# Attention and ternary FFN on one core: the FFN of a batch moved into the next batch's step

## What is computed

```python
# attention: 16 heads of 16 channels
q = xn @ Wq.T; latent = xn @ Wkv_down.T; k = latent @ Wk_up.T; v = latent @ Wv_up.T
att = softmax(where(mask, q k / 4, -inf))     # band of 64 keys, and the first 4 keys ("sinks")
y = (att v) @ Wo.T
# ffn: two "bit linears", weights ternarized
def bitlinear(x, w):
    n = layer_norm(x)                         # over the row
    return n @ (sign(round(w / mean|w|)) * mean|w|).T
h = gelu(bitlinear(xn, w_fc))                 # (256, 1024) a batch
ffn = bitlinear(h, w_proj)                    # (256, 256) a batch
```

## Time and profile before

| | |
|---|---|
| median of 3 runs | 192.17 us (191.29 to 192.31) |
| the profiled execution | 193.13 us, of which the span of its instructions 191.2 us |
| TensorE (PE) busy | 147.9 us (77%), 2166 products |
| DVE busy | 111.3 us (58%) |
| ACT busy | 83.8 us (44%) |
| POOL busy | 34.0 us (18%) |
| mean granted TensorE clock | 0.911 of full |
| the chain that ended last | PE 54%, DVE 26%, ACT 10%, issue 3%, DMA 3% of the span |

### The profile page before, as it was taken

How to read it: one execution, slowest core, us unless ns; L and a number is a source line. 1 busy time by engine, 2 the same in 40 slices (tenths; PEclk the granted TensorE clock), 3 DMA queues, 4 the chain that set the end, 5 groups by cost and what they waited for, 6 DMA issues and landing times.

```text
span 191.2 us, 4928 instructions
## 1 busy us (share of the span) xinstructions
PE 147.9 (77%) x2166; PEld 103.6 (54%) x2166; DVE 111.3 (58%) x190; ACT 83.8 (44%) x124; POOL 34.0 (18%) x64
## 2 busy tenths in 40 slices
PE   1627930979799991998999929997999289989823
PEld 1415710446678760547888604476887144778711
DVE  0359799985750467657814675658025777380461
ACT  1656710456936222347762223369532205596100
POOL 6421491000073000200460001101210002003000
PEclk9999995599979999799999985999999759999987
DMA  5997000010000000040000000300000003000001
GB/s 172 304 347 186 23 2 0 3 54 6 0 0 3 3 3 0 24 140 3 3 2 3 3 0 0 110 3 3 0 3 3 2 3 110 0 3 0 3 3 55
DMA packets 7969, 7.61 MB, mean 40 GB/s; under 512 B 2564, under 2 KB 7592, under 8 KB 7848
## 3 DMA queue, kind: packets, MB, share of 16 engines
q1 hardware_dynamic: 6236, 6.05, 10.4%
q10 hardware_dynamic: 1712, 1.25, 2.1%
HBM read 6.24 MB, written 1.05 MB: 38 GB/s over the span
## 4 chain that ended last, share of the span: by engine, by line
PE 54%; DVE 26%; ACT 10%; issue 3%; DMA 3%; ACTq 1%; POOL 1%
PE acc L1000 8%; PE ring L937 7%; DVE rden L695 7%; PE ring L867 7%; PE aux L1036 6%; PE acc L1026 4%; ACT gh L407 3%; DVE mx L650 3%; DMA wvu_r<-in_L_attn_Wv_up 3%; PE ring L980 3%; PE ring L920 3%; DVE KL L630 3%; PE aux L855 2%; PE ring L989 2%; PE acc L1018 2%
## 5 line engine op out<-in xcount | busy, mean ns | idle before, releaser
L920 PE MATMUL ring<-mask,idb 128*128 128x384 bf16 (+1 forms) x48 | 15.4, 410 | 18.5 <-DVE vs L642 16.3
L421 ACT ACTIVATE E<-ring,un 128x1024 f32<-128x1024 f32 x16 | 17.7, 1112 | 6.2 <-PE ring L980 6.2
L655 DVE TENSOR_REDUCE mx<-ring 128x4 f32<-128x768 f32 x16 | 14.9, 953 | 6.0 <-PE ring L925 5.5
L625 DVE SCALAR_TENSOR_TENSOR Q<-qh,rowlo,ring 128x1024 f16<-128x1024 f16 x4 | 5.1, 1277 | 21.9 <-ACT qh L434 21.9
L452 ACT ACTIVATE yhT<-y 128x256 f16<-128x256 f32 x8 | 3.3, 416 | 31.9 <-DVE y L700 31.9
L920 PEld LDWEIGHTS ring<-mask,idb 128*128 128x128 bf16 x48 | 3.6, 108 | 22.1 <-ACT V L444 10.9
L1000 PE MATMUL acc<-prT,gh 128*128 128x256 f16 x64 | 15.5, 285 | 0.0
L1000 PE MATMUL acc<-prT,glo 128*128 128x256 f16 x64 | 15.3, 284 | 0.0
L317 POOL TENSOR_TENSOR ob<-att,xff 128x512 f32<-128x512 f32 x3 | 3.8, 1263 | 56.7 <-issue 37.8
L394 ACT ACTIVATE gl<-ring,a 128x1024 f32<-128x1024 f32 x8 | 8.9, 1113 | 10.0 <-PE ring L937 9.9
L689 DVE SCALAR_TENSOR_TENSOR glo<-ring,gam_r,gh 128x1024 f16<-128x1024 f32 x8 | 9.9, 1279 | 5.8 <-ACT gh L407 5.8
(11 more groups left out here) (187 smaller groups left out, 390.5 us busy)
## 6 DMA issues: line engine op xcount, KB each, us to landing
wfc_r<-in_L_ffn_w_fc SPq DMA_DIRECT2D x1, 1024.0 KB, 8.1
wpr_r<-in_L_ffn_w_proj SPq DMA_DIRECT2D x1, 1024.0 KB, 10.4
xres<-in_L_attn_x SPq DMA_DIRECT2D x4, 256.0 KB, 2.8
out<-ob SPq DMA_DIRECT2D x4, 256.0 KB, 2.1
bias<-in_c_bias SPq DMA_DIRECT2D x1, 825.0 KB
xin<-in_L_attn_x ACTq DMA_DIRECT2D x3, 256.0 KB, 2.8
wq_r<-in_L_attn_Wq ACTq DMA_DIRECT2D x1, 256.0 KB, 3.3
xin<-in_L_attn_x SPq DMA_DIRECT2D x1, 256.0 KB, 3.8
```

The lines of the kernel that those rows point to most:

```text
L421: nc.scalar.activation(E[:, 2 * gp:2 * gp + 2, 2 * tp:2 * tp + 2, :].rearrange("p g t q -> p g (t q)"), slot("p2", b, r)[:], ACT.Exp, scal ...
L655: nc.vector.tensor_reduce(out=o, in_=src[:, :, 0:2 * (T - BLK)].rearrange("p a (t k) -> p a t k", t=2), axis=AX.X, op=ALU.max).then_inc(re ...
L920: nc.tensor.matmul(s[:, a, 0:n * len(heads)].rearrange("p (t k) -> p t k", t=len(heads)), idb[:], mask[:].unsqueeze(1).to_broadcast([P, le ...
```

## The change

Step b keeps the back part of batch b and the front part of b + 1, but the FFN in it is now that of batch a = b - 1. Step 0 has no FFN; in its place the ternary weights are made there. The last step has two FFNs: that of batch 2 and that of batch 3. In detail:

- The row operands `xhT`, `xlT` get three buffers, and `a1` two, since they are read one step later.
- PE's order in steps 1 and 2: `maxima_transposed`, rows, sinks, `window_scores` 0, 1, latents, `window_scores` 2, `fc_tile(a, 0)`, `window_scores` 3, `fc_tile(a, 1)`, q, values 0, k, values 1, v, `hidden_transposed(a, 0)`, round 0 of the maxima, `hidden_transposed(a, 1)`, round 1, `second_product(a, 0)`, rounds 2 and 3, `second_product(a, 1)`, rounds 4 and 5, `output_product(b)`. The last product moves from ahead of round 3 to behind round 5, and into `acc`.
- `ORDER` follows, so the ring's waits change: q waits for `gelu(a, 0)`, the second transposed tile for `sink_values`, round 1 for the low half of tile 0, round 3 for that of tile 1.
- ACT and DVE: `hidden` behind the last exponential, `hidden_high` behind `values_moved`, `hidden_low` ahead of maxima 0 and 1. POOL's `residual(b - 1)` and `result(b - 1)` stand at the end of step b, and ACT's `attended(b)` behind the FFN's evacuation.
- Weights: the magnitudes of `w_fc` are summed on DVE and of `w_proj` on ACT (they swap), the two means are taken apart, both `is_lt` compares are on POOL; `first_ternary` on DVE stands in step 0 ahead of the queries, `second_ternary` behind maxima 0, with their transposes on ring places of their own.
- The last step ends with `second_product` of batch 3 in a ring place; DVE adds the attention part into `xff` and then scales and adds per tile, and SP stores two halves.

```diff
-                fc_tile(b, 0)
-                fc_tile(b, 1)
                 maxima_transposed(b)
-                if more:
-                    transposed_rows(b + 1)
+                if f < B:
+                    transposed_rows(f)
                 sink_scores(b)
-                hidden_transposed(b, 0)
-                hidden_transposed(b, 1)
                 window_scores(b, 0)
                 window_scores(b, 1)
-                if more:
-                    latents(b + 1)
-                second_product(b, 0)
+                if f < B:
+                    latents(f)
                 window_scores(b, 2)
-                second_product(b, 1)
+                if b:
+                    fc_tile(a, 0)
                 window_scores(b, 3)
...
+                if f < B:
+                    q_products(f)
+                    values(b, 0)
+                    k_products(f)
+                    values(b, 1)
+                    v_products(f)
+                    if b:
+                        hidden_transposed(a, 0)
+                        window_maxima(f, 0)
+                        hidden_transposed(a, 1)
+                        window_maxima(f, 1)
+                        second_product(a, 0, acc[:, 0:C])
+                        window_maxima(f, 2)
+                        window_maxima(f, 3)
+                        second_product(a, 1, acc[:, C:2 * C])
+                    else:
+                        first_ternary()
+                        window_maxima(f, 0)
+                        window_maxima(f, 1)
+                        second_ternary()
+                        window_maxima(f, 2)
+                        window_maxima(f, 3)
+                    window_maxima(f, 4)
+                    window_maxima(f, 5)
+                    output_product(b)
+                else:
+                    values(b, 0)
+                    hidden_transposed(a, 0)
+                    values(b, 1)
+                    hidden_transposed(a, 1)
+                    fc_tile(b, 0)
+                    fc_tile(b, 1)
+                    second_product(a, 0, acc[:, 0:C])
+                    second_product(a, 1, acc[:, C:2 * C])
+                    output_product(b)
+                    hidden_transposed(b, 0)
+                    hidden_transposed(b, 1)
+                    last_bank = take("F2", b)
+                    for i in range(TT_):
+                        second_product(b, i, last_bank[:, i, 0:C])
```

The last step on DVE, and POOL's loop:

```diff
+                    normalised(b, 0)
+                    hidden_low(a, 0)
+                    attended_low(b, 0)
+                    normalised(b, 1)
+                    hidden_low(a, 1)
+                    attended_low(b, 1)
+                    hidden_stats(b, 0)
+                    hidden_stats(b, 1)
+                    last_attended(b)
+                    hidden_low(b, 0)
+                    hidden_low(b, 1)
+                    last_result(b, 0)
+                    last_result(b, 1)
...
+            def last_attended(b):
                 wait(dve, mm_wo, b)
+                wait(dve, ld_res, b)
+                wait(dve, o_ok, b - 1)
...
+                first_scale(b)
                 if b + 2 < B:
                     row_factors(b + 2)
+                if b:
+                    second_scale(b - 1)
+                    residual(b - 1)
+                    result(b - 1)
+            second_scale(B - 1)
```

More of the change, by code:

```diff
@@ new lines, in maxima_slots, with score_slots, fc_slot, hidden_slot @@
+        def maxima_slots(f, rounds):
+            return [("f_p1", f, r, [(red1, f, r + 1)] + ([(red1s, f, 1)] if r == 5 else [])) for r in rounds]
+        def score_slots(b, rounds):
+            return [("p2", b, r, [(ex, b, r + 1)]) for r in rounds]
+        def fc_slot(a, i):
+            return [("fc", a, i, [(gelu, a, i + 1)])]
+        def hidden_slot(a, i):
+            return [("t2T", a, i, [(glo_ok, a, i + 1)])]
+        ORDER = rows_slot(0) + projection_slots(0) + maxima_slots(0, range(6))
@@ L567, in weight_sums @@
+                nc.vector.tensor_scalar(pthr[:, at], thr[:, at], 0.5, None, ALU.mult).then_inc(w_thr, 1)
+                dve.wait_ge(means, 2 * n + 1)
+                if n == 0:
+                    nc.vector.reciprocal(gam_r[:], gam_c[:]).then_inc(means, 1)
+                else:
+                    nc.vector.tensor_scalar(gam2[:], gam[:, 0:1], gam[:, 1:2], None, ALU.mult).then_inc(means, 1)
             def weight_sums():
-                dve.wait_ge(ld_wp, 16)
-                nc.vector.tensor_reduce(out=wsum[:, 1, :], in_=flat(wpr_r).rearrange("p (a k) -> p a k", k=C), axis=AX.X, op=ALU.add,
-                                        apply_absolute_value=True).then_inc(w_abs, 1)
+                dve.wait_ge(ld_wf, 16)
@@ L730, in _ @@
             keys_low(0)
-            first_ternary()
             sink_values(0)
             for r in range(6):
-                if r == 3:
-                    second_ternary()
+                if r == 4:
+                    weight_means(1)
                 maxima(0, r)
@@ L751, in _ @@
                 if b + 2 < B:
                     row_norm(b + 2)
[L753 to L769 removed]
+                if b:
+                    hidden_stats(a, 0)
+                    hidden_stats(a, 1)
+                else:
+                    first_ternary()
@@ new lines, in _ @@
+                if f < B:
+                    queries(f)
+                    normalised(b, 0)
+                    keys_low(f)
+                    attended_low(b, 0)
+                    normalised(b, 1)
+                    sink_values(f)
+                    if b:
+                        hidden_low(a, 0)
+                    maxima(f, 0)
+                    if b:
+                        hidden_low(a, 1)
+                    else:
+                        second_ternary()
+                    maxima(f, 1)
+                    attended_low(b, 1)
+                    for r in range(2, 6):
+                        maxima(f, r)
+                    row_maxima(f)
+                else:
+                    normalised(b, 0)
+                    hidden_low(a, 0)
+                    attended_low(b, 0)
+                    normalised(b, 1)
+                    hidden_low(a, 1)
+                    attended_low(b, 1)
+                    hidden_stats(b, 0)
[5 more added lines that the diff above has]
+                    last_result(b, 1)
@@ L1032, in output_product @@
                 wait(pe, yl_ok, b)
+                if b:
+                    wait(pe, ffn_ok, b - 1)
+                o = acc if b + 1 < B else aux
                 for j in range(TT_):
@@ L1044, in _ @@
             k_products(0)
-            weight_totals()
+            weight_totals(0)
             v_products(0)
```

311 lines of the change are left out of this document (149 added, 162 removed).

## The result

The changed kernel took **200.42 us** in the median of four runs (198.26 to 201.62), against 192.24 (191.29 to 195.07) for the kernel before beside it: a ratio of 1.041, 95% interval 1.027 to 1.054. It is slower, as forecast, but by 8.2 us and not by 2.7, and the time lies above the range of 189.5 to 199.0.

The account below looks back on a forecast made before the run. PE bounds M (`maxima_transposed` starts) to R (DVE's first reciprocal); behind R it waits on DVE, then bounds again. M3 153.0 plus tail 41.2, less 0.3, gives span 193.9; plus 0.97, 194.9 us; range 189.5 to 199.0.

Parts of the forecast that it names:

- One hit, 1.1: Head: POOL's second compare slows one of two small DVE instructions in `row_maxima`, adding 1.1 us.
- 0.9 for half of a low stretch: Step 0, M to R: PE's idling ahead of M lowers the clock, adding 0.9 us, bounds 0 and 1.7.
- the 0.97 from the span to the median: End of the sum: 0.97 us added to the span of 193.9 to reach the median of the runs.
- the hole stays: Steps 1 and 2, behind R: PE still idles 3.4 us until `sink_values` frees a ring place.
- The wait of about 1 us for `glo`: Steps 1 and 2, behind the hole: PE waits about 1 us for DVE's `glo` before round 1.
- the 12.7 at full clock: Step 0, M to R: 6.9 + 5.8 = 12.7 us without FFN, before any low clock.
- the wait of q: Steps 1 and 2, M to R: q's place waits about 1.8 us for ACT's Gelu.
- The rival that the clock falls there: Steps 1 and 2, wait ahead of q: a low stretch costs 1.7 us a step, 199 us; chance 0.14.
- The rivals with less low clock: Whole kernel: denser maxima part holds 2.4 GHz, 186.5 to 188, chance 0.22; one or two low stretches less, about 192, 0.17.
- The table drain: Rival: each ACT table load costs about 1.4 us more, 199 us in all; chance 0.02.
- The bounds of the transfer: Tail: `xres` of batch 3 loads behind POOL's residual and result, delaying `last_attended`; bounds 0 and 4.5 us.
- 0.3 less for rounds counted with 1.1: Sum: 0.3 us taken off because score rounds were counted with 1.1 instead of 1.02 us.

Follow-up runs that it names:

- a_pool: Changed kernel with POOL's second compare held until the row maxima of batch 0 are done: 196.47 us, ratio 1.016 to the kernel before.
- a_head: Changed kernel with POOL's second compare held back and eight unread products ahead of the first `maxima_transposed`: 196.24 us, ratio 1.008 to the kernel before.
- a_warm: Changed kernel with 24 unread products in PE's wait for `sink_values` in steps 1 and 2: median 203.11 us, profiled execution 197.05.
- b_warm: Kernel before with 24 unread products ahead of round 2 of the maxima in steps 0 to 2: 188.35 us, ratio 0.975.
- a_xres: Changed kernel with two buffers for `xres`, so batch 3's load no longer waits for batch 2's residual: 195.45 us, ratio 1.011 to the kernel before.
- a_dense0: Changed kernel with POOL's second compare late and two groups of eight unread 512-column products around `window_scores` 3 in step 0: 204.72 us, ratio 1.062.
- a_best: Changed kernel with POOL's compare late, two `xres` buffers, `fc_tile(a, 1)` behind v, unread products in PE's waits: 181.93 us, ratio 0.935 to the kernel before.

## Why the prediction missed

Three terms of the sum failed, and the mechanism around them held. "One hit, 1.1" for POOL beside `row_maxima` measured 3.0 us in two hits. "0.9 for half of a low stretch" in step 0 measured 2.2. And the 0.97 from the span to the median should have been 1.9, with slower executions than the profiled one on top.

**The direction and the pieces were right.** By M1 the change was 10.6 us ahead (74.65 against 85.25), steps 1 and 2 lost 4.1 of it, and the tail with its two FFNs cost 13.1 more than before: 6.6 us slower in the span, with the signs of the forecast at each place. Most of the signs it named showed: PE waits 1.80 for Gelu ahead of q, the hole stays (3.37), `last_attended` waits for DMA, PE idles over 4 us ahead of the last products. Two did not. The wait of about 1 us for `glo` behind the hole is filled by the transposes, which take 1.94 at the low clock. And M came at 37.9, 74.7, 115.9 and 157.0 instead of 36.6, 72, 112 and 153, later at each place.

**Head: the term "one hit, 1.1" (+1.3).** The bounds given were 0 and 2 x 1.15; measured were two hits of 1.5, 3.0 us, outside even the upper bound, and a_pool took exactly these 3.0 away. Two errors are in it. I counted one hit because in the earlier trace rows one of two instructions was hit; that the other, 0.21 at 27.46, went free under the same compare told nothing of the next two. And the price of 1.15 came from a row of another shape. The rest of the head was 0.7 better than forecast (34.8 in a_pool against 35.5), which hid part of the error. The Trainium skill (GPSIMD Engine Reference, section Specifications) names besides instructions with two SBUF inputs those in a 2-port mode as contending. By it, the row at 35.87, with a single fp32 input in SBUF and a bf16 output there, can only be of that kind, which the prediction had left out; whether it ran in such a mode no run here shows. With it the count would have been two. The Trainium skill (SBUF — State Buffer, section SBUF: two separate sides) has the side that starts second blocked for the whole instruction of the other. By that `mm` would have ended no sooner than POOL's compare, at 37.52; it ended at 35.84, so the trace doesn't bear this out.

**Step 0: "0.9 for half of a low stretch" (+1.5).** The clock was 0.51 from 29 to 43, 5 us of it behind M0, and cost 2.2 us: a_head, where it ended at 35, took 12.9 instead of 15.1, so the 12.7 at full clock was right to 0.2. The bounds of 0 and 1.7 went by stretches of 3.4 us, as in the earlier trace rows; here it was one of 14 x 0.49 x 2 = 13.7. It is tempting to blame the wait of 5.08, twice the 2.6 I had counted on, but a_pool, with 1.99, did no better. What the forecast lacked was that a low stretch that begins in the head can last far into step 0; what sets its length stays open.

**Steps 1 and 2.** M to R 18.3 for 18.0, the wait of q as forecast. The rival that the clock falls there (199 us, chance 0.14) is closest in time and didn't happen: the clock is 1.00 from 71 to 81, and q starts at full pace. R to M 23.0 and 22.8 for 22.5: the low stretch cost 1.5 to 1.7 (a_warm) where 1.4 was taken, and POOL's result once more slowed `mm`, 0.65 instead of 0.19:

```profile
114.08 1.26 POOL L336 TENSOR_TENSOR ob<-att,xff 128x512 f32<-128x512 f32 x1
...
114.73 0.65 DVE L700 TENSOR_TENSOR mm<-mx,smx 128x32 f32<-128x32 f32 x1
```

Step 2 has the same 0.65. I had counted POOL's residual and result only as what `attended` waits for, and not as neighbours of `row_maxima`.

**The rivals with less low clock** (0.22 and 0.17) ask for a cause that isn't there: more work around a hole of the same length did not keep the clock up. Work inside the hole did, as b_warm and a_warm show.

**The table drain** (0.02): the Gelu starts 0.02 us behind the load (85.94 against 84.64 + 1.28), as in the earlier trace rows. The Exp load at the start of the last two steps cost nothing either.

**Tail (-0.4).** 41.2 against 40.8. The bounds of the transfer, 0 and 4.5, had the whole wait at their end, and that is where the forecast stood; a_xres gives back 4.8, with the clock behind the wait.

**Sum.** The "0.3 less for rounds counted with 1.1" was wrong by its whole size: in the changed kernel score rounds follow each other by 1.1.

**From the span to the median (+1.6).** I added 0.97, the distance in the runs of before. In each execution of after the time lies 1.8 to 1.9 above its own span, which is 0.9 more than that, and the profiled span of 197.8 is 0.75 under the middle of the four (196.4, 197.8, 199.3, 199.8): the two longer ones ran at a mean clock of 0.889 and 0.887. 0.889 over 199.3 us is 6.6 us more at 1.2 GHz than in the profiled one. So 3.9 + 1.6 = 5.5, the whole miss. Some 2.6 of it go with low clock that was priced too low (1.5 in step 0, 0.75 in the other executions, 0.4 in the two steps behind the holes), 1.3 are the head with its contention, and 0.9 that I added the distance of a median where the profiled execution's own, 1.93, was the right one; the rest are the small terms of the table.

**The range.** Its upper end stood for the clock falling ahead of q. It left no room for a term outside its bounds, and two terms were: the contention and the low stretch of step 0.

## What to carry to other kernels

Ask of every hole in PE not only how long it is but what runs behind it: here a hole of 3.4 us cost another 1.5 at half clock in each step, and 2.5% of the time was to be had by putting products that nobody reads into it. When a step is moved to the end of a loop, follow the buffers of its smallest transfers to the tail: one 256 KB buffer cost 4.8 of the change's loss. And when work moves to GpSimd, lay its interval over DVE's smallest SBUF instructions ahead of a wait, let the upper bound count each as hit, and price it by a row that was hit.

## What the runs showed of the hardware that was not expected

- A DVE instruction on 128 x 32 elements in SBUF took 1.70 us beside a POOL `tensor_scalar` of 5.44 us, and 0.19 without it; one with a single SBUF input was hit as hard as one with two (1.69 against 0.18).
- Around M0, PE stayed at 1.2 GHz for 21 to 24 us although it was busy for 87 to 90% of them (a_dense0, a_pool); other executions of the same kernel (a_pool) are some 7 us shorter. What decides between the two courses is open.
- 24 products of 256 columns inside each hole held the clock at 2.4 GHz through the stretches behind it (b_warm, a_warm), and with nearly all holes filled six executions lay within 0.7% (a_best), where the kernel before took 192.41 to 196.21 us on the same chip.
